# First attention without a block of its own for its weights: loads in order of need, value copies between the first roundings, spare copy in mid-stage

## The reference

```python
c_q = h @ w_down_q.T                      # latents, 128 wide
c_kv = h @ w_down_kv.T
q = (c_q @ w_up_q.T).reshape(b, s, H, DH).transpose(0, 2, 1, 3)   # H = 16, DH = 64
k = (c_kv @ w_up_k.T).reshape(b, s, H, DH).transpose(0, 2, 1, 3)
v = (c_kv @ w_up_v.T).reshape(b, s, H, DH).transpose(0, 2, 1, 3)
q = _apply_rope_subspace(q, DR)
k = _apply_rope_subspace(k, DR)
attn = jax.nn.softmax(jnp.einsum('bhqd,bhkd->bhqk', q, k) * scale, axis=-1)
out = jnp.einsum('bhqk,bhkd->bhqd', attn, v)
out = out.transpose(0, 2, 1, 3).reshape(b, s, H * DH) @ w_out.T + residual
```

## Time and profile before

| | |
|---|---|
| time, median of 3 runs | 2163.25 us (2158.48 to 2170.83) |
| profiled execution, own time | 2154.38 us |
| its span, first to last instruction | 2152.7 us |
| PE busy | 1887.4 us (88%) |
| POOL busy | 1333.0 us (62%) |
| DVE busy | 1255.7 us (58%) |
| ACT busy | 900.7 us (42%) |
| mean granted TensorE clock | 0.954 of full |

### The profile page before, as it was taken

The page is one execution under the profiler, slowest core; times in us unless marked ns, Lnnn a source line. Parts: engine busy times, 40 slices in busy tenths (PEclk is TensorE's granted clock), DMA queues, the critical chain, the costliest instruction groups (busy, mean ns, idle before and its releaser), DMA issues. The chain is left out here.

```text
span 2152.7 us, 35007 instructions
## 1 busy us (share of the span) xinstructions
PE 1887.4 (88%) x12812; PEld 1313.1 (61%) x12812; DVE 1255.7 (58%) x1748; ACT 900.7 (42%) x1537; POOL 1333.0 (62%) x854
## 2 busy tenths in 40 slices
PE   5996599999999999999999837788884899997898
PEld 4886344544545454454545426666663899997898
DVE  5774466667565666656566425766762666565443
ACT  5884244334343433434343304333321455554455
POOL 3643388778686877868687613455453766666533
PEclk9998699999999999999999968999997999999999
DMA  4323213232221323222132230222224333333222
GB/s 133 108 99 134 59 42 76 52 96 59 67 72 33 96 52 96 59 70 70 36 92 55 55 126 31 60 69 64 69 65 146 91 85 82 77 84 75 34 48 40
DMA packets 82464, 159.15 MB, mean 74 GB/s; under 512 B 14704, under 2 KB 64112, under 8 KB 76400
## 3 DMA queue, kind: packets, MB, share of 16 engines
q1 hardware_dynamic: 67312, 133.79, 22.2%
q0 software_dynamic: 14592, 18.40, 5.4%
q10 hardware_dynamic: 432, 5.24, 0.6%
HBM read 81.23 MB, written 44.17 MB: 58 GB/s over the span
## 5 line engine op out<-in xcount | busy, mean ns | idle before, releaser
L1123 ACT ACTIVATE a_pr<-a_pT 128x1024 f32<-128x1024 f32 x256 | 262.0, 1023 | 428.4 <-PE a_pT L946 428.4
L1156 POOL TENSOR_TENSOR a_total<-a_total,a_pr 128x1024 f32<-128x1024 f32 x128 | 319.7, 2498 | 149.8 <-ACT a_pr L1123 149.7
L1028 DVE TENSOR_REDUCE a_row_max<-a_pG 128x2 f32<-128x1024 f32 x256 | 309.2, 1220 | 149.7 <-PE a_pG L920 149.6
L2039 DVE TENSOR_TENSOR c_h_lo<-c_h,c_h_hi 128x256 fp32r<-128x256 f32 x288 | 210.6, 749 | 192.9 <-ACT c_h_hi L2018 181.2
L959 PE MATMUL a_pA<-a_pr,a_v 128*64 128x512 f32 x1024 | 277.1, 619 | 0.1
L2018 ACT ACTIVATE c_h<-c_pU,c_b_c 128x256 f32<-128x256 f32 x288 | 138.7, 482 | 232.5 <-PE c_pU L103 232.3
L1156 POOL TENSOR_TENSOR a_total<-a_pr 128x1024 f32<-128x1024 f32 x64 | 151.7, 2370 | 56.4 <-ACT a_pr L1123 56.1
L1137 POOL TENSOR_TENSOR a_by_cos<-a_by_cos,a_swapped 128x1024 f32<-128x1024 f32 x64 | 155.9, 2435 | 47.4 <-DMA a_swapped<-a_by_sin 47.4
L1022 DVE TENSOR_TENSOR a_by_sin<-a_pG,a_sin 128x1024 f32<-128x1024 f32 x64 | 78.4, 1225 | 141.0 <-PE a_pG L103 136.2
L1144 POOL TENSOR_TENSOR a_qk_lo<-a_by_cos,a_qk_hi 128x1024 fp32r<-128x1024 f32 x64 | 158.8, 2481 | 2.3 <-ACT a_qk_hi L1093 2.3
L2075 POOL DMA_INDIRECT out_x<-c_y,c_ids x72 | 115.2, 1600 | 40.7 <-DVE c_y L2047 21.5
(11 more groups left out here) (253 smaller groups left out, 4897.9 us busy)
## 6 DMA issues: line engine op xcount, KB each, us to landing
a_swapped<-a_by_sin SPq DMA_DIRECT2D x256, 128.0 KB, 2.3
a_inv_by_head<-mid_inverses SPq DMA_DIRECT2D x32, 512.0 KB, 5.9
c_x_t<-mid_rows SPq DMA_DIRECT2D x37, 272.0 KB, 2.8
mid_latents<-f_c_parts SPq DMA_DIRECT2D x8, 1024.0 KB, 3.9
a_latent_parts<-mid_latents SPq DMA_DIRECT2D x8, 1024.0 KB, 7.2
d_raw<-in_weights SPq DMA_DIRECT2D x3, 2048.0 KB, 7.9
c_raw<-in_weights SPq DMA_DIRECT2D x3, 2048.0 KB, 7.9
f_x_t<-in_x SPq DMA_DIRECT2D x8, 512.0 KB, 3.8
```

The source lines that it names most:

```text
L1028: nc.vector.reduce_max(row_max[:, u % 2, :, t], pair[:], AX.X).then_inc(read, 1)
L1123: nc.scalar.activation(pr[:, n % RP, :, :], pT[:], ACT.Exp, scale=SCALE).then_inc(exp_done, 1)
L1156: nc.gpsimd.tensor_tensor(total[:, u % 2, :, :], before, pr[:, n % RP, :, :], ALU.add).then_inc(summed, 1)
L2039: nc.vector.tensor_tensor(h_lo[:, m % RH, :], h[:, m % RH, :], h_hi[:, m % RH, :], ALU.subtract).then_inc(h_lo_done[m % RH], 1)
```

## The change

The first block goes. Its work moves to the head of the four programs of the second block, with semaphores of its own for each load (`raw_in` per projection, `tables_in`, `masks_in`, `wo_in`). SP's order becomes: raw q, raw k, latents of batch 0, sin, cos, raw v, ident, neg_blocks, swap(0), swap(1), part_for(0), wo. ScalarE rounds each projection as it comes in. VectorE clears the semaphores, makes the three remainders, waits for the tables, and rotates. TensorE waits for two remainders ahead of the first product and for the third ahead of the values, for the masks ahead of the first transpose, for `fills` behind it, and for wo in the first output projection. ScalarE's first value copies now alternate with the first two `qk_high`. The raw weights keep their place in SBUF through the stage. The spare copy is issued in unit 16, behind `spread(3)`, and no longer at the end.

```diff
--- before.py
+++ after.py
@@ -688,7 +688,10 @@
         v = sb("v", [P, NT, NP, 2, DH])
         row_max = sb("row_max", [P, 2, 2, DH])
 
-        loaded = sem("loaded")
+        raw_in = {n: sem(f"raw_{n}_in") for n in names}
+        tables_in = sem("tables_in")
+        masks_in = sem("masks_in")
+        wo_in = sem("wo_in")
         w_split = sem("w_split")
         w_lo_done = sem("w_lo_done")
         fills = sem("fills")
@@ -715,43 +718,7 @@
         part_in = sem("part_in")
         stored = sem("stored")
 
-        with ExitStack() as ctx2:
-            raw = {n: ctx2.enter_context(nc.sbuf_tensor(f"a_raw_{n}", [P, f], F32)) for n, (_, f) in names.items()}
-            with nc.Block() as block:
-                @block.sync
-                def _(sp):
-                    for n, (src, _) in names.items():
-                        sp.dma_start(raw[n][:], src).then_inc(loaded, 16)
-                    for dst, src in ((ident, ident_d), (neg_blocks, neg_blocks_d), (cos, rope_c), (sin, rope_s), (wo, wo_t)):
-                        sp.dma_start(dst[:], src).then_inc(loaded, 16)
-
-                @block.scalar
-                def _(act):
-                    act.wait_ge(loaded, 16 * (len(names) + 5))
-                    for n in names:
-                        nc.scalar.copy(w_hi[n][:], raw[n][:]).then_inc(w_split, 1)
-
-                @block.vector
-                def _(dve):
-
-                    for s in spent:
-                        dve.sem_clear(s)
-                    for i, n in enumerate(names):
-                        dve.wait_ge(w_split, i + 1)
-                        nc.vector.tensor_tensor(w_lo[n][:], raw[n][:], w_hi[n][:],
-                                                ALU.subtract).then_inc(w_lo_done, 1)
-                    dve.wait_ge(w_lo_done, len(names))
-
-                @block.gpsimd
-                def _(pool):
-                    nc.gpsimd.memset(ones[:].bitcast(F32), 1.0).then_inc(fills, 1)
-                    nc.gpsimd.memset(row_max[:], 0.0).then_inc(fills, 1)
-                    nc.gpsimd.memset(row_of[:], 0.0).then_inc(fills, 1)
-                    pool.wait_ge(fills, 3)
-                    for g in range(GROUP):
-                        nc.gpsimd.memset(row_of[:, g, g:DH:GROUP], 1.0).then_inc(fills, 1)
-                    pool.wait_ge(fills, 3 + GROUP)
-
+        raw = {n: sb(f"raw_{n}", [P, f]) for n, (_, f) in names.items()}
         x_t = sb("x_t", [P, NT, D])
         c = sb("latent_parts", [P, 4, S], F32R)
         by_cos = sb("by_cos", [P, 2, 2, S])
@@ -863,10 +830,21 @@
                         sp.dma_start(inv_by_head[64 * h:64 * h + 64, :, :],
                                      inverses[g % 2, h, :, :].unsqueeze(0).to_broadcast([64, GROUP, S])).then_inc(inv_in, 16)
 
+                def raw_for(n):
+                    sp.dma_start(raw[n][:], names[n][0]).then_inc(raw_in[n], 16)
+
+                raw_for("q")
+                raw_for("k")
                 latents_for(0)
+                for dst, src in ((sin, rope_s), (cos, rope_c)):
+                    sp.dma_start(dst[:], src).then_inc(tables_in, 16)
+                raw_for("v")
+                for dst, src in ((ident, ident_d), (neg_blocks, neg_blocks_d)):
+                    sp.dma_start(dst[:], src).then_inc(masks_in, 16)
                 swap(0)
                 swap(1)
                 part_for(0)
+                sp.dma_start(wo[:], wo_t).then_inc(wo_in, 16)
                 for u in range(UNITS):
                     b, p = divmod(u, NP)
                     if u + 2 < UNITS:
@@ -878,10 +856,12 @@
                         part_for(b)
                     if p == NP - 3 and b + 1 < B:
                         latents_for(b + 1)
+                    if u == 2 * NP:
+                        sp.wait_ge(stored, 16)
+                        sp.dma_start(tokens(x1, B), tokens(x1, 0)).then_inc(spare_done, 16)
                 spread(UNITS // GROUP - 1)
                 store(B - 1)
                 sp.wait_ge(stored, 16 * B)
-                sp.dma_start(tokens(x1, B), tokens(x1, 0)).then_inc(spare_done, 16)
                 sp.wait_ge(spare_done, 16)
 
             @block.tensor
@@ -971,6 +951,8 @@
 
                 def project_out(b, t):
                     pair, done = begin("out", b, t)
+                    if not b and not t:
+                        pe.wait_ge(wo_in, 16)
                     pe.wait_ge(norm_done, NP // 2 * (b + 1))
                     ts = slice(t * P, (t + 1) * P)
                     for p in range(NP):
@@ -978,13 +960,17 @@
                                                 start=(p == 0), stop=(p == NP - 1))
                     last.then_inc(done, 1)
 
+                pe.wait_ge(w_lo_done, 2)
                 for u in (0, 1):
                     queries_and_keys(u)
+                pe.wait_ge(w_lo_done, 3)
                 for i in range(2):
                     values(0, 0, i)
                 for t in range(NT):
                     scores(0, t)
+                pe.wait_ge(masks_in, 32)
                 transpose_maxima(0)
+                pe.wait_ge(fills, 3 + GROUP)
                 for u in range(UNITS):
                     for t in range(NT):
                         if t == NT - 1 and u + 1 < UNITS:
@@ -1055,10 +1041,19 @@
                     dve.wait_ge(part_in, 16 * (b + 1))
                     nc.vector.tensor_tensor(x_t[:, t, :], pair[:, 0, 0:D], x_t[:, t, :], ALU.add).then_inc(read, 1)
 
+
+                for s in spent:
+                    dve.sem_clear(s)
+                for i, n in enumerate(names):
+                    dve.wait_ge(w_split, i + 1)
+                    nc.vector.tensor_tensor(w_lo[n][:], raw[n][:], w_hi[n][:], ALU.subtract).then_inc(w_lo_done, 1)
+                dve.wait_ge(tables_in, 32)
                 for u in (0, 1):
                     rotate(u)
+                dve.wait_ge(fills, 3)
                 for t in range(NT):
                     maximum(0, t)
+                dve.wait_ge(masks_in, 32)
                 negate(0)
                 for u in range(UNITS):
                     g = u // GROUP - 1
@@ -1109,10 +1104,12 @@
                         wait_filled(act, "out", (u - RA) // NP, NT - 1)
                     nc.scalar.copy(att[:, u % RA, :], pA[:]).then_inc(att_out, 1)
 
-                qk_high(0)
-                qk_high(1)
+                for n in names:
+                    act.wait_ge(raw_in[n], 16)
+                    nc.scalar.copy(w_hi[n][:], raw[n][:]).then_inc(w_split, 1)
                 for i in range(2):
                     values(0, 0, i)
+                    qk_high(i)
                 for u in range(UNITS):
                     for t in range(NT):
                         n = NT * u + t
@@ -1156,6 +1153,12 @@
                     nc.gpsimd.tensor_tensor(total[:, u % 2, :, :], before, pr[:, n % RP, :, :],
                                             ALU.add).then_inc(summed, 1)
 
+                nc.gpsimd.memset(ones[:].bitcast(F32), 1.0).then_inc(fills, 1)
+                nc.gpsimd.memset(row_max[:], 0.0).then_inc(fills, 1)
+                nc.gpsimd.memset(row_of[:], 0.0).then_inc(fills, 1)
+                pool.wait_ge(fills, 3)
+                for g in range(GROUP):
+                    nc.gpsimd.memset(row_of[:, g, g:DH:GROUP], 1.0).then_inc(fills, 1)
                 rope(0)
                 qk_low(0)
                 rope(1)
```

## The result

The changed kernel took a median of 2143.81 us over six runs (2141.72 to 2155.21), the kernel before 2163.72 over six (2158.48 to 2170.83): a ratio of 0.9909, 95% interval 0.9884 to 0.9934, or 19.9 us less, where 20.9 were forecast. The profiled execution took 2143.61, its span 2141.9. So there are two questions: do the edges give what the sum said, and where are the other 9 us of the profile.

The account below looks back on a forecast made before the run. The 50 us ahead of 252.4 were taken as a chain of latencies, the loop behind as bound by its own cycle. 11.5 + 5.7 + 3.7 = 20.9 us off 2163.25 gave 2142.3 us, range 2133 to 2154.

Parts of the forecast that it names:

- The loads: Stage start, SP's queue: loads land one by one at 385 KB per us, latents at 210.0, v at 212.6.
- What is late next: Stage start: v's load, through its remainder on VectorE, holds rotate(0), which moves from 226.44 to 214.9, 11.5 us.
- The clears: Stage start, VectorE: clearing 50 semaphores ends before the first remainder's rounding does, so it costs nothing.
- The value copies: ScalarE between the first roundings: first values copied ahead of unit 1's rounding, first scores earlier by net 5.7 us.
- The spare copy: End of stage: without the copy there, the block ends on its last store, 3.7 us saved.
- The collision: Unit 16: moved copy delays swap(19) 0.3 us past its cover, taken as 0, at most 1.9; rival's chance 0.04.
- The loads together: Rival, stage start: loads all land at 213.5, rotate(0) at 219.9, gain only 15.9 us; chance 0.08.
- The clock: Rival, TensorE in the loop: stays at the low clock, 6.4 us lost per unit, kernel slower; chance 0.03.
- The sum: Whole kernel: 11.5 + 5.7 + 3.7 = 20.9 us less, median 2142.3 us.
- the loop runs as before: Loop over 64 units behind the first exponential: bound by its own cycle, unchanged, only 17.2 us earlier.
- 6 us of scatter: Bounds on the median: the 12.4 us spread of the runs adds some 6 us on each side.

Follow-up runs that it names:

- e4: The changed kernel with rotate(0) ahead of the remainder of v on VectorE: 2140.90 us, ratio 0.9897 to the kernel before.
- e10: The kernel of e4 again, on the third chip beside e9: 2133.98 us, ratio 0.9887 to the kernel before.
- e9: The changed kernel, unchanged, second trace, on a third chip: 2136.60 us against 2157.26, ratio 0.9895.
- e1: The kernel before with the spare copy alone moved to unit 16, both blocks kept: 2161.35 us against 2164.63, ratio 0.9985.
- e5: The kernel before, unchanged, run for a second trace: 2160.09 us.
- e8: The kernel before, unchanged, third trace, on a third chip: 2157.26 us.
- e2: The changed kernel with ScalarE's old order, both query and key roundings ahead of all value copies: 2150.79 us, ratio 0.9937 to the kernel before.
- e7: The changed kernel with the spare copy made twice in unit 16, the second issued when the first landed: 2145.37 us against 2160.38 before, ratio 0.9921.
- e3: The changed kernel with ScalarE waiting for latents, projections, tables and masks before any rounding: 2148.86 us, ratio 0.9923 to the kernel before.
- e6: The kernel before with the load of batch 0's latents moved into the first block: 2157.53 us against 2160.38, ratio 0.9988.

## Why the prediction was right, point by point

- **The loads.** Forecast were q at 206.0, the latents at 210.0, v at 212.6; they came at 205.4, 210.5 and 213.1. The rate of 385 KB per us, read off before's queue, was too high: from q to v 2560 KB took 7.7 us, 332 KB per us. That the sum held to 0.5 us was luck in part: q came 0.6 sooner (3.3 us after its issue instead of 3.8), and the two errors offset each other. The Trainium skill's 358 GB/s ("DMA: Bandwidth & Descriptors", Specifications) gives, as an estimate, v at 213.3 and was nearer here; the 332 KB per us are 340 GB/s, below it, as before's 394 were above.
- **What is late next.** Named right: v's load, through its remainder, not the latents that TensorE waits for. TensorE came 12.8 us earlier (forecast 13.5) and rotate(0) 11.0; e4 and e10 take the remainder away and 1.6 us (e4 against the first trace of the changed kernel) and 1.3 us (e10 against e9) more come through. Forecast 11.5; mean of before's shape (before, e1, e5, e8) 24.2 less mean of after's (after, e2, e7, e9) 12.9 is 11.3.
- **The clears** of 50 semaphores cost nothing: the first remainder started at 206.53, as its rounding ended.
- **The value copies.** Forecast 5.7, measured 5.8 (e2 against the changed kernel). Every milestone of that chain was late or early by at most 0.7.
- **The spare copy.** 3.7 forecast, 3.7 measured, in all nine traces with it moved. The collision: 0.3 us beyond the cover were forecast and taken as nothing; rope(19) waited 0.72, so the cover was read too large, but the next spread still came 68.7 us behind this one, as in before. e7 shows what a delay of SP costs with the cover gone, 4.7.
- **The rivals.** The loads together (e3 makes all roundings wait for the last of them): 4.3 us to rotate(0), forecast 5.0. The clock: the first query products of the loop ran at the low level (0.63 us each to 237.7), and the loop's first matmul at the high one (0.40) is at 238.82, in unit 0's second tile. The level had been up once before, at 215.0 (0.39 each), and was down again at 218.45 (0.63). In before the loop's first high one is at 253.53, 1.2 us behind the first exponential; here it is 3.3 behind. From the first exponential to the first spread it took 68.5 us, where before has 67.2; but over all traces it is 67.2 to 68.3 with the old start (mean 67.8) and 67.2 to 68.9 with the new (mean 68.1), so what the clock took is some 0.3 us, within the scatter. It didn't stay low.
- **The sum.** 20.9 forecast; edges 20.7 by means over the traces of the table; medians 19.9 in the first comparison and 20.7 on the third chip.
- **What the prediction lacked.** It said that "the loop runs as before", and gave 6 us of scatter to each side without knowing where the scatter lives. Most of it lives in the second attention (the store of batch 5 comes after 316 to 325 us, that of batch 6 after 32 or 40), less in the stage at hand (1016 to 1020 us without e7), whose loop did run as before on average. Anyone who had judged the change by the two spans, 10.8 apart, would have called it half of what it is.

## What stays open

Why TensorE's instructions come in bursts in batch 6. All four traces on the first chip (e1 to e4) had the 40 us, none of the seven on the other two chips, and the changed kernel had both values, so the edit doesn't decide it; whether the chip or the single execution does isn't shown. "issue" ahead of bursts of 1 to 14 matmuls would fit a late supply of instructions. But the profile lists two queues for instructions, and in none of the five traces does either move anything from the first burst to the last, so a fetch from memory at that time isn't what they show.

What e2 and e3 lost ahead of the store of batch 5 (5 and 8 us) is another thing, though it looks alike in the table. TensorE has no idle time put down to issue there. In each of their batches 1 to 5 the mean granted clock is 0.92, where before and the changed kernel have 0.96, and the same matmuls take longer because the high level comes later in the batch. Batch 1 of e2 as a window, and one row of it, then the same of the changed kernel:

```profile
1372.67:1416.02 43.35, 36.63 (x408) 28.23 (x400) 28.69 (x61) 13.84 (x29) 20.16 (x28) 0.92 0.21 66
...
1380.84 2.09 PE L1450 MATMUL b_pA<-d_own,b_kT 32*128 32x256 f32 x16
```

```profile
1371.25:1412.47 41.22, 35.42 (x408) 27.76 (x400) 28.27 (x61) 13.93 (x29) 20.33 (x29) 0.96 0.24 69
...
1379.16 1.15 PE L1449 MATMUL b_pA<-d_own,b_kT 32*128 32x256 f32 x16
```

e8, the kernel before, has two such batches too (43.1 us at 0.92 and 43.8 at 0.88), so this isn't the edit's either. Why the clock came up later in them is open.

## What to carry to other kernels

A block of its own for loads cost little by itself (half a us here, e6); it cost what couldn't be issued until it ended (4.9 us), and the wait of its one gate for the slowest load (4.3, e3). When loads are put in order of need, the order of the consumer's own program counts as much: one remainder ahead of rotate(0) held back 1.3 to 1.6 us of what TensorE had won. And compare traces by landmarks on both sides of the edit, not by spans: the edges repeat within a us, while one untouched place took 32 or 40.

## What the runs showed that I had not expected

A DMA from memory to memory of 512 KB landed 3.7 us after its issue alone, and 7.0 behind a spread of 512 KB (e7). And a stretch of 32 short matmuls took 1.1 or 6.2 us in the same program, with the granted clock falling to 0.50 behind it: 8 us to the store of that batch, and still 5.9 to the store of the next.
